# A state-space layer and an int8 matmul: transposes on an idle TensorE in the first chunk, and new tables for the order of all engines

## The reference

```python
x = x + s6(layernorm(x), A_log, D, x_proj_w, dt_proj_w, dt_proj_b)
x = x + quantized_matmul(layernorm(x), weight_q, weight_scale) + bias
# s6:
A = -exp(A_log)                                   # 512 x 16 states
d_rank, B, C = split(x @ x_proj_w.T)              # 64, 16, 16
delta = softplus(d_rank @ dt_proj_w.T + dt_proj_b)
h[t] = exp(delta[t] * A) * h[t-1] + delta[t] * B[t] * x[t]    # per channel, per state
y[t] = sum_n h[t, :, n] * C[t, n] + x[t] * D
# quantized_matmul: rows scaled to int8 by their largest value, times int8 weights
```

## Time and profile before

| what | value |
|---|---|
| median of 3 executions | 2774.99 us (2774.4 to 2779.16) |
| the profiled execution | 2778.11 us |
| its span from first to last instruction | 2776.4 us |
| TensorE busy | 2738.9 us, 99% |
| VectorE busy | 2710.0 us, 98% |
| ScalarE busy | 2690.4 us, 97% |
| GpSimd busy | 2691.1 us, 97% |
| `times_c`, GpSimd, 511 times | 4727 ns each in the mean |
| load of a quarter of C's rows, 128 times | 5.3 us to landing in the median |
| load of a diagonal, 192 times | 3.9 us |
| `add_c`, 31 times | 10.2 us |

### The profile page before, as it was taken

One profiled execution on the slowest core, in us unless ns is written; L12 is line 12 of the kernel. 1 busy time (PEld: TensorE's weight loads), 2 busy tenths in 40 slices (PEclk: granted clock), 3 DMA queues, 4 the chain that ended last, 5 costly groups with the idle time before them and its releaser, 6 DMA issues.

```text
span 2776.4 us, 59139 instructions
## 1 busy us (share of the span) xinstructions
PE 2738.9 (99%) x22516; PEld 2513.1 (91%) x22516; DVE 2710.0 (98%) x2801; ACT 2690.4 (97%) x4927; POOL 2691.1 (97%) x981
## 2 busy tenths in 40 slices
PE   7999999999999999999999999999999999999998
PEld 6889999999999999999999989999999999899987
DVE  6999999999999999999999999999999999999987
ACT  8899999999999999999999999999999999999995
POOL 4899999999999999999999999999999999999998
PEclk9999999999999999999999999999999999999999
DMA  5245454445454554554553535545544545455361
GB/s 187 99 105 128 106 147 119 127 119 124 126 153 96 134 130 110 144 135 111 119 130 119 153 96 134 130 113 140 138 108 119 130 119 153 100 132 129 95 155 49
DMA packets 271653, 344.33 MB, mean 124 GB/s; under 512 B 174917, under 2 KB 174917, under 8 KB 251018
## 3 DMA queue, kind: packets, MB, share of 16 engines
q1 hardware_dynamic: 250538, 275.54, 32.7%
q0 software_dynamic: 20832, 65.02, 14.5%
HBM read 253.60 MB, written 103.16 MB: 129 GB/s over the span
## 4 chain that ended last, share of the span: by engine, by line
PE 85%; POOL 5%; DMA 3%; issue 3%; DVE 2%; ACT 1%; SPq 1%; DVEq 0%; POOLq 0%; ACTq 0%
PE Y L850 28%; PE PB L825 20%; PE PB L828 18%; PE PM L950 4%; PE PM L909 4%; PE PM L890 4%; POOL A L599 4%; PE Y L846 3%; DMA CB<-c_rows 3%; PE PM L918 2%; PE PM L880 2%; DVE A L982 1%; DMA out<-C 1%; POOL C L616 1%; DVE X L990 0%
## 5 line engine op out<-in xcount | busy, mean ns | idle before, releaser
L599 POOL TENSOR_TENSOR A<-A,CB 128x2048 f32<-128x2048 f32 x511 | 2336.1, 4727 | 56.0 <-ACT CAR L671 41.4
L982 DVE TENSOR_TENSOR_SCAN A<-A,CAR,PB 128x512 f32<-128x512 f32 x1536 | 1832.3, 1256 | 12.3 <-ACT A L664 5.1
L664 ACT ACTIVATE A<-DEL,an 128x512 f32<-128x512 f32 x2048 | 1327.6, 713 | 7.3 <-PE Y L850 6.8
L850 PE MATMUL Y<-idf,A 128*128 128x128 f32 x8192 | 1095.3, 273 | 1.0 <-POOL A L599 0.9
L850 PEld LDWEIGHTS Y<-idf,A 128*128 128x128 f32 x8192 | 934.6, 141 | 20.1 <-issue 17.2
L683 ACT ACTIVATE DB<-XN,BC 128x512 f32<-128x512 f32 x1344 | 896.8, 712 | 10.7 <-DVE XN L1012 10.7
L828 PE MATMUL PB<-idf,DB 128*128 128x128 f32 x5376 | 767.1, 274 | 12.4 <-DVE A L982 7.8
L825 PEld LDWEIGHTS PB<-DG,XN 128*128 128x128 f32 x5632 | 689.7, 192 | 72.7 <-issue 49.9
L825 PE MATMUL PB<-DG,XN 128*128 128x128 f32 x5632 | 729.0, 276 | 3.8 <-DVE A L982 3.5
L828 PEld LDWEIGHTS PB<-idf,DB 128*128 128x128 f32 x5376 | 625.4, 142 | 57.0 <-issue 21.6
L982 DVE TENSOR_TENSOR_SCAN A<-A,PB 128x512 f32<-128x512 f32 x512 | 587.6, 1201 | 20.8 <-PE PB L828 11.3
(11 more groups left out here) (92 smaller groups left out, 1379.3 us busy)
## 6 DMA issues: line engine op xcount, KB each, us to landing
CB<-c_rows SPq DMA_DIRECT2D x128, 1024.0 KB, 5.3
DG<-b_diag SPq DMA_DIRECT2D x192, 256.0 KB, 3.9
X<-in_x SPq DMA_DIRECT2D x31, 1024.0 KB, 7.4
out<-X SPq DMA_DIRECT2D x31, 1024.0 KB, 8.7
out<-bias_rows POOLq DMA_DIRECT2D x31, 1024.0 KB, 8.6
out<-C POOLq DMA_DIRECT2D x31, 1024.0 KB, 10.2
b_diag<-DG SPq DMA_DIRECT2D x2, 1536.0 KB, 11.3
b_diag<-BC SPq DMA_DIRECT2D x192, 2.0 KB, 3.0
```

The source lines that it names most:

```text
L599: gp.tensor_tensor(A[s % NA][:, :, :], A[s % NA][:, :, :], CB[:, s % (4 * NG), :].unsqueeze(1).broadcast_to([128, KB, L]), ALU.mult).then_ ...
L664: act.activation(A[s % NA][:, g, :], DEL[k % 2][:, g, :], ACT.Exp, scale=an[:, g, n:n + 1])\
L850: i = pe.matmul(Y[j][:, g * 128:(g + 1) * 128], A[s % NA][:, g, j * 128:(j + 1) * 128], idf[:, :], is_transpose=True, start=False, stop=(n ...
L982: dve.tensor_tensor_scan(A[s % NA][:, g, :], A[s % NA][:, g, :], PB[(4 * s + g) % NPB][:, :], init, ALU.mult, ALU.add).then_inc(s_scan, 1)
```

## The change

Two things change. First, TensorE gets a step `warm` with twelve blocks of 8 transposes of the unit matrix into PM, in chunk 0 only; the first block waits until B and C have been copied out of PM. Nobody reads what they write, and no semaphore counts them.

```diff
+            def warm(p, i):
+                if p == 0:
+                    if i == 0:
+                        pe.wait_ge(s_bce, 1)
+                    for _ in range(8):
+                        pe.transpose(PM[:, 0:128], idf[:, :], idf[:, :])
...
-            run(idle=idle, x_t=x_t, x_p=x_p, d_t=d_t, b_c=lambda p, i: b_c(p), dl_t=dl_t, q_t=q_t, q_mm=q_mm, tb=tb, th=th)
+            run(idle=idle, warm=warm, x_t=x_t, x_p=x_p, d_t=d_t, b_c=lambda p, i: b_c(p), dl_t=dl_t, q_t=q_t, q_mm=q_mm, tb=tb, th=th)
```

Second, nearly all numbers of PLACES and FIRST are new; LAST stays. Of these tables, three lines:

```diff
-        "load_c": (230, 412, 805, 942),
-        "load_g": (-115, 13, 13, 164, 884, 885),
+        "load_c": (107, 189, 717, 1001),
+        "load_g": (35, 113, 310, 426, 1034, 1035),
...
+        "warm": (-25231, -24121, -23794, -23737, -22003, -21960, -15900, -15080, -13326, -13116, -12141,
+        -11743),
```

More of the change, by code:

```diff
@@ L30 @@
+        679, 684, 686, 723, 759),
+        "delta": (-462, -443, -424, -401),
+        "dl_t": (-273, -230, -204, -182),
+        "du": (-4, -1, 4, 11),
+        "gather": (1103, 1105, 1124, 1124),
         "idle": (2244, 2663, 2696, 3192),
-        "inv": (1173,),
+        "inv": (1168,),
         "last_p": (25000, 25001),
@@ L107 @@
+        783, 968),
+        "centre": (1388, 1430, 1430, 1514),
+        "d_t": (-33957, -33012, -29651, -25933),
+        "decay": (-39568, -34134, -31458, -28450, -27901, -27860, -27860, -27860, -27860, -27860, -27860,
[4 rows of a table added]
+        "delta": (-74157, -60979, -54203, -54032),
+        "dl_t": (-24857, -24740, -24740, -24089),
+        "du": (-1253, -1155, -842, -842),
+        "gather": (1098, 1111, 1111, 1119),
+        "inv": (1208,),
         "late": (-12995, -12985, 100, 200),
         "load": (16363,),
-        "load_c": (-34082, -7485, -6765, 435),
@@ L141 @@
[L141 to L147 removed]
+        "load_c": (-27496, -8988, -6862, 534),
+        "load_g": (-26047, -9268, -8644, -7488, -7488, -7486),
+        "log0": (-125282,),
+        "put_x": (1491,),
+        "q_mm": (1852, 1858, 1871, 1900),
+        "qt_out": (1693, 1755, 1788, 1796),
@@ L148 @@
+        -11743),
+        "weights": (-100, 300),
+        "x_p": (-35568, -35568, -35568, -35123),
+        "x_t": (-56389, -46593, -38630, -37735),
+        "xn": (-86957, -86154, -83910),
+        "xn_p": (-50358,),
+        "xp_out": (-75048,),
         "xt_d": (-1709, -1567),
-        "xt_out": (-62861, -58231, -55646, -44834),
+        "xt_out": (-82258, -81938, -80443, -76619),
 }
```

167 lines of the change are left out of this document (73 added, 94 removed), and 42 rows, old and new, of tables (FIRST, PLACES).

## The result

| | before | changed |
|---|---|---|
| median | 2774.99 us (2774.4 to 2779.16) | 2762.73 us (2762.24 to 2764.95) |
| profiled execution | 2778.11 us | 2762.24 us |
| its span | 2776.4 us | 2760.5 us |

The ratio of the times is 0.9955, 95% interval 0.9941 to 0.997: the change makes the kernel 12.3 us faster. I gave faster 0.38 and no difference 0.47.

A forecast was written before the change was run, and what follows sets the result against it. It held every engine over 98% busy in the middle, leaving gains to opening stalls and GpSimd's waits for C's rows. Terms -2.0 (opening), -1.4 (chunks 1 to 4), -1.6 (steady) made -5.0 us: median 2770.0 us, range 2763 to 2781.

The forecast's parts named there:

- The steady chunks: Steady part after the opening: earlier centre instructions and loads on GpSimd and SP, worth 1.0 to 3.0 us, taken as 1.6.
- Late rows: Steady part: most of GpSimd's 10.0 us of waits for rows of C in 2000 us go, worth 1.6 us.
- The compute orders: Steady part: longer table loads only move ScalarE's steps, and ScalarE is not the bound, so 0.
- The opening: -2.0 us: Start of the kernel: clock, order, blocks and first cast together save 2.0 us; bounds -6 and +2.5 us.
- Blocks +0.3, clock -1.0: Opening, TensorE: idle transposes delay the start by 0.3 us; the held clock saves VectorE 1.0 us of waits.
- First cast +1.4: Opening, VectorE: the first cast now falls inside GpSimd's first product and waits it out, costing 1.4 us.
- Order at 75 to 97 us, -2.7: Opening: reordered projection steps for chunk 1 remove VectorE's stalls, -3.1 us, with 0.4 us given back.
- Chunks 1 to 3: -1.4 us: Chunk 1 to chunk 4: the add of C issued some 9 us earlier spares ScalarE's wait, -1.4 us, at worst 0.
- Rival 1: Second cast finds GpSimd idle and late landings go wholly: 2766 us or less, down to 2763; chance 0.15.
- Rival 2: Opening gives nothing: blocks run at the lower clock or second cast waits a product; 2773.5 us; with Rival 4 0.20.
- Rival 4: Landings stay late and GpSimd's backlog takes back the opening's gain: 2775 us; chance 0.20 together with Rival 2.
- Rival 3: Steady chunks: unit 14's diagonal lands late behind SP's new order, up to 2798 us; chance 0.15 with similar mishaps.

The follow-up runs named there:

- rowscentre: Kernel before with load_c and store_c new and GpSimd's step, bias transfer and centre instructions one product of C earlier: 2769.03 us, ratio 0.9974.
- comprowsdiag: Added to rowscentre: new PLACES of TensorE, ScalarE and VectorE and the diagonals' new numbers (load_g, store_g): 2772.86 us, ratio 0.9983 to before.
- places: Kernel before with the new PLACES on all engines, old FIRST, no idle transposes: 2764.87 us, ratio 0.9958.
- nowarm: Changed kernel with blocks of no transposes, both tables new: 2764.2 us, ratio 0.9953 to before.
- again: Changed kernel run once more without edit, on another chip: 2764.39 us, ratio 0.9946 to before.
- castnowarm: Changed kernel with VectorE's two chunk 0 casts moved (behind scans 5 and 39) and no idle transposes: 2759.72 us, ratio 0.994 to before.
- rows: Kernel before with only load_c and store_c new, so quarters 1 and 2 of C's rows load earlier: 2770.64 us, ratio 0.9986.
- sp: Kernel before with new PLACES for SP's steps alone, every compute engine in its old order: 2920.49 us, ratio 1.0506.
- diag: Kernel before with only the diagonals' numbers (load_g, store_g) new: 2952.88 us, ratio 1.0637.
- sppool: Kernel before with new PLACES of SP and GpSimd; TensorE, VectorE and ScalarE keep the old order: 2992.28 us, ratio 1.0781.
- warm16: Changed kernel with blocks of 16 transposes instead of 8: 2768.93 us, ratio 0.9975 to before.
- cast: Changed kernel with VectorE's two chunk 0 casts moved, behind scan 5 and behind scan 39: 2759.58 us, ratio 0.994 to before.
- olddiag: Changed kernel with the diagonals' load_g and store_g at their old numbers: 2768.1 us, ratio 0.9975 to before.

## Why the prediction was wrong, step by step

**The steady chunks: the step that failed.** I wrote that in the middle "every engine is over 98% busy" and "so new orders cannot gain much there", and took 1.6 us. In the profiles chunks 4 to 29 became 9.3 us shorter. One term of this was mis-sized, and one was put at 0 without a look at the lists.

- *Late rows.* I saw GpSimd's longest wait reach VectorE with 1.88 of 2.64 us, let the others count for little, and took 1.6 us. rowscentre has no late row and holds just the part that I had named (the early quarters, and the centre instructions one product earlier). Against before it is 7.2 us faster by the ratio and 8.4 us in the profiled spans. Of these, 3.2 us lie in chunks 4 to 27, which I had let count for little, and 2.0 in chunks 28 and 29, where the 1.88 us lies that I had seen: 5.2 us for my 1.6. The others are 0.4 us before the first scan, 1.3 in chunk 0 and 1.5 in chunks 1 to 3. I also took "the lower part, for the reason given on the median". That reason was wrong: the executions of before spread over 7 to 9 us and those of rowscentre over 3, so late landings make the spread, and the median pays as well.
- *The compute orders.* "The longer table loads only move ScalarE's steps; ScalarE is not the bound, so 0." From rowscentre to comprowsdiag, which adds the compute orders and the diagonals' numbers, chunks 4 to 27 fall from 2030.9 to 2027.1 us, 3.8 us; from rowscentre to places the ratio falls by 0.0016, 4.4 us. The table changed TensorE's and VectorE's lists as well, and I never priced them, since TensorE "has no idle" in the earlier trace rows. That reading can't carry the step: in the same stretch TensorE is busy for 499.98 of 500 us in rowscentre and for 499.80 in the faster kernel. Which list or wait brings the 3.8 us is open.

The record speaks against one candidate. The weight loads' wait for PM falls from 7.5 us in rowscentre to 0.8 in the changed kernel, but not where the time is gained. Means over the six sequences from chunk 4 to chunk 27, us per chunk (one third chunk of rowscentre took 85.23 us, the other five 84.89):

| chunk of its sequence | first | second | third | fourth |
|---|---|---|---|---|
| rowscentre, length | 83.71 | 84.95 | 84.95 | 84.88 |
| changed, length | 83.35 | 84.95 | 84.79 | 84.77 |
| rowscentre, wait for PM | 0.13 | 0.45 | 0.45 | 0.22 |
| changed, wait for PM | 0 | 0.13 | 0 | 0 |

Waits under 0.15 us are not shown. The second chunk loses 0.32 us of this wait and gains nothing; the first loses 0.13 and gains 0.36, more than half of the 0.6 us of a sequence. Two other waits fall as well between 500 and 2500 us, ScalarE's for XN from 7.4 to 1.7 us and GpSimd's for CAR from 6.8 to 4.1 us; neither was tested.

**The opening: -2.0 us.** The size was about right. From places to the changed kernel the ratios fall from 0.9958 to 0.9953, 0.9955 and 0.9946 (nowarm, changed, again), 0.8 to 3.3 us, with intervals that overlap. By the profiles, chunk 0 took 86.7 to 89.2 us in twelve with the old FIRST (87.8 in the mean), and 84.6, 84.6, 84.6, 86.0 and 86.2 us in five with the new one (85.2): 2.6 us less.

- *Blocks +0.3, clock -1.0.* Right in the parts: 0.9 us for a block, the 24 matmuls in 2.84 us against "2.7". The worth was misplaced. Where the clock falls before the cast, as in nowarm, nothing is slower, since the cast covers that time; where it falls behind the cast, as in again, chunk 0 is 1.4 us longer; with the cast out of the way it is 1.5 us (castnowarm). The clock also falls at holes shorter than the 2.5 us that I went by: 1.84 us in again, and 1.93 us, ending at 83.23 us, at the third slow stretch of before.
- *First cast +1.4.* Right: 2.06 us instead of 0.67, since it now starts inside the product. Moved ahead of the product, it is 0.67 again.
- *Second cast 0.* It went from 2.83 to 1.57 us, 1.3 better, inside the bounds that I kept (-2.2 to +2.3).
- *Order at 75 to 97 us, -2.7.* Right: the holes of 0.85, 1.48 and 0.75 us went, and one of 0.60 stayed.

**Chunks 1 to 3: -1.4 us.** Measured -1.8 in the profiles. But the move of the add of C (it had stood behind the second product of chunk 2, not the first, as I wrote) was not needed for most of it: in rows and rowscentre the add stands where it stood (issued at 221.38 and 221.18 us), ScalarE waits for it no more, and chunks 1 to 3 take 255.1 us, 1.5 of the 1.8 us. Before, a megabyte load of C's rows was issued 0.08 us ahead of the add, which landed after 13.9 us; without that load beside it, it landed after 11.0 and 11.5 us.

**Rival 1** (everything goes well, 2766 down to 2763, chance 0.15) came nearest, for another reason. **Rival 2** was wrong in that blocks and second cast did no harm. **Rival 4** did not happen. **Rival 3** did not decide, but its mechanism is real and dearer than I had it: in sp and diag the same loads land after TensorE wants them, and the price is 145 and 178 us. My estimate for the changed kernel, 7.6 us from issue to use, was 7.2 to 9.3 when measured (median 8.3), with a landing of 4.2 to 6.6 us for this load. In sp TensorE comes 1.6 us after the issue, so the changed kernel has 6.7 us more; in sppool, where only GpSimd's list is new as well, it is 5.7 to 7.5 us and nothing waits for a diagonal.

With the steady term at its 9.3 us the sum would have been -12.7 us, 2762.3 us as a median, 0.4 us below the result. That it comes so near is partly luck: the sum was made on profiled executions, and these are 15.9 us apart. The last chunk, which I had put at 0 with 1 us either way, is 1.1 us longer.

## What to carry to other kernels

When all engines are over 98% busy, don't take the busy share as a bound on what a new order can gain. Take the time of equal units of work (here four chunks), and compare the fastest with the others: what repeats in all is order, what varies is lateness. A sum of small waits names candidates and no cause: look whether the unit that lost the wait also lost the time, and don't add the waits of an engine and of its weight loads, which can be the same time.

A spread of a kernel's executions that is larger than its neighbours' is a hint that transfers land late; here moving them earlier removed the spread (8 to 3 us) and the loss together. Parts of a jointly tuned table can't be priced one by one: here the same two lines were worth 4 us in one order and 91 in the other, and each half of the table alone made the kernel slower.

## What the runs showed of the hardware

A cast of 128x1024 from int32 to bf16 on VectorE takes 0.67 us when GpSimd stands idle, and 1.57, 2.06, 2.83 and 3.16 us (in places) when it starts inside one of GpSimd's products of 4.5 us, ending some 0.5 us behind the product. The scans are not slowed: in the changed kernel 28 of them take 31.38 us, nearly all of it beside products, 1.12 us each, and three ahead of the first product take 3.44 us. The Trainium skill, "SBUF — State Buffer", section "Who interferes with whom", says that a cast in a two-port mode and a GpSimd instruction lock each other out for a whole instruction, and that the one issued first wins. The traces agree for the side that they show, the product being first: 0.67 us for each cast that starts outside a product (the first of before and of warm16, both in cast), longer for each inside one.

The column stores of 2 KB (`b_diag<-BC`) landed after 3.0 us in the median before and after 5.4 us in the changed kernel, where they follow a load of 1 MB on the same queue. That this load delays them is not shown: in olddiag, where none stands just ahead of them, it was 8.0 us. The loads of the diagonals wait for them. I had not expected that 2 KB would take longer to land than the megabyte's 4.8 us:

```profile
CB<-c_rows SPq DMA_DIRECT2D x128, 1024.0 KB, 4.8
DG<-b_diag SPq DMA_DIRECT2D x192, 256.0 KB, 5.0
...
b_diag<-BC SPq DMA_DIRECT2D x192, 2.0 KB, 5.4
```
